# Splitting the last output projection of a state-space mixer around the first cross-attention tiles, and moving two LayerNorms two tiles later

## The chip, the cores and the metric

The kernel runs on one core of a Trainium2 chip. The metric is device time in microseconds (us) of the whole launch, the median of several runs. A core has four computing engines, each with its own instruction queue worked off in order: TensorE (PE in the profile; its weight loads are PEld), VectorE (DVE), ScalarE (ACT) and GpSimd (POOL). SyncE (SP) only issues transfers here. Engines wait for each other through semaphores.

## What is computed

A decoder layer with post-normalisation over x of shape (2, 2048, 512) in float32: a state-space mixer, a cross attention on a context of 77 rows, and a feed-forward part in which 16 slots per batch attend to all tokens, pass through 16 experts, and are attended to by the tokens.

```python
x = _layernorm(x + mixer(x, W_in, conv_w, conv_b, A_param, dt_bias, W_out))
x = _layernorm(x + cross_attention(x, ctx_1024, q_w, ..., o_b))
x = _layernorm(x + slots_and_experts(x, slot_query, ..., e_b2))
```

The end of the mixer is `out.reshape(b, s, -1) @ W_out.T`, then residual and LayerNorm. In the cross attention, `q = x @ q_w + q_b` with 16 heads of 32 columns, softmax over the 77 rows of context under a causal mask, the weighted values, and `@ o_w + o_b`, again with residual and LayerNorm.

## The kernel before, in words

The sequence of 2048 is cut into 16 chunks of 128 positions (`CHUNKS`, numbered 0 to 15; `END` is 15), and a chunk covers both batches (`BATCH` is 2). The cross attention goes over 32 tiles of 128 tokens: tiles 0 to 15 are batch 0, tiles 16 to 31 batch 1. The program is one block in which each engine's order is written out by hand in `cross_rows`: first a Python loop over chunks 0 to 14 of the mixer, then a hand-ordered seam that mixes the end of chunk 15 with the start of tiles 0 and 1, and then `tiles(engine, step)`, which calls `step(t, ...)` for every tile. Tiles 0 to `MIXER_OVER` are written out one by one, then a hardware loop takes two tiles per turn up to tile 13, then four tiles are written out, then a second loop and the last two tiles.

Mixer parts at the seam (`mixer_parts`). `project_out` (line 776) multiplies the rated output of a chunk with W_out, one group of matrix products per batch; for chunk 15 the two results lie in the PSUM banks that the cross stage calls TO (batch 0) and SLOT (batch 1). `residual` (line 834) adds x on DVE, once per batch, and counts `res_done`. `norm` computes mean and reciprocal deviation of a chunk for both batches on DVE: two bn_stats (line 602), then a chain of tiny operations, each waiting for the last (lines 615 to 631 and 842). `normalise` (line 796) applies them on ACT with two activations; `store` (line 713) writes the chunk to memory on SP's queue, from where `load` (line 941) fetches the tiles.

Cross parts of a tile t, in the order of the dependencies: `turn_x1` (PE, 959), `take_x1T` (ACT, 1062), `queries` (PE, 968), `take_queries` (DVE, 1126), `score` (PE, 981), `take_scores` (DVE: maximum 1118 and subtraction 1120, with a mask addition 1115 at tiles 0 and 16 alone), `exponents` (ACT, 1066), `denominators` (DVE: sum 1148, reciprocal 1151), `normalise` (POOL, 1189), `turn_probs` (PE, 988), `take_probsT` (ACT, 1090), `weigh_values` (PE, 997), `take_yT` (ACT, 1106), `project_out` (PE, 1007), `residual` (DVE, 1175), `norm` (DVE, 643 to 660), `scale_rows` (ACT, 1096), `turn_x2` (PE, 1028), `take_x2T` (ACT, 1072), `slot_scores` (PE, 1036), `slot_maxima` (DVE, 1135 to 1144), `slot_exponents` (ACT, 1079 and 1082), `turn_slots` (PE, 1044), `take_slotsT` (ACT, 1101), `weigh_tokens` (PE, 1056), `add_tokens` (DVE, 1163).

They are software-pipelined. `step(t)` on DVE is: `add_tokens(t-2)`, `take_queries(t+1)`, `take_scores(t+1)`, `slot_maxima(t-1)`, `denominators(t+1)`, `slot_sums(t-1)`, `residual(t)`, `norm(t)`. On ACT it begins with `take_probsT(t)` and ends with `scale_rows(t)`. On PE it begins with `turn_probs(t)`, `turn_x1(t+2)`, `weigh_values(t)`, `turn_x2(t-1)`, `score(t+1)`, and ends with `queries(t+2)` and `weigh_tokens(t-1)`. On POOL it is `add_bias(t+1)` and `normalise(t+1)`.

In the kernel before, both batches of the last `project_out` come right before tile 0's `turn_probs` on PE; both residuals and the norm of chunk 14 come right before `step(0)` on DVE, and the norm of chunk 15 in `step(1)`, after `take_queries(2)`. The rows of chunks 14 and 15 are scaled on ACT in steps 1 and 2 (`LATE_ROWS`) and stored in steps 2 and 3 (`LATE_STORES`). After the tiles, the experts stream their weights (2 MB units) from memory.

Of the kernel before, what the change touches and what calls it, by code (L numbers as in the profile page):

```python
# [24 lines left out]
BATCH, SEQ, D = 2, 2048, 512  # L25
TOKENS = BATCH * SEQ
TILES = TOKENS // P
CHUNKS = SEQ // P
# [117 lines left out]
def wait_later(eng, sem, value):  # L146

    if not isinstance(value, int) or value > 0:
        eng.wait_ge(sem, value)
# [522 lines left out]
def mixer_parts(nc, io, hold, st):  # L672
# [96 lines left out]
                                        start=False, stop=True, skip_group_check=True)  # L769
        last.then_inc(s["y_done"], 1)  # L770

    def project_out(pe, c):
        for b in range(BATCH):
            pe.wait_ge(s["yT_done"], 2 * c + b + 1)
            for g in range(GROUPS):
                last = nc.tensor.matmul(outputs(c)[b], yT[:, b, g * P:(g + 1) * P], wout[:, g, :], start=(g == 0), stop=(g == GROUPS - 1))  # L776
            last.then_inc(s["out_done"], 1)
# [47 lines left out]
        for b in range(BATCH):  # L825
            nc.vector.tensor_tensor(yT[:, b, :], Y[:], rateT[c % 2][:, b * GROUPS:(b + 1) * GROUPS, :].rearrange("p g t -> p (g t)"), ALU.mult).then_inc(s["yT_done"], 1)  # L826

    def residual(dve, c):
        u = c % 2
        dve.wait_ge(x_arrived[u], 16 * (c // 2 + 1))  # L830
        wait_later(dve, s["x1_done"], c - 1)
        for b in range(BATCH):
            dve.wait_ge(s["out_done"], 2 * c + b + 1)
            nc.vector.tensor_tensor(xr[u][:, b, :], outputs(c)[b], x_in[u][:, b, :], ALU.add).then_inc(s["res_done"], 1)  # L834

# [44 lines left out]

MIXER_OVER = 7
LATE_ROWS = {1: CHUNKS - 2, 2: CHUNKS - 1}
LATE_STORES = {2: CHUNKS - 2, 3: CHUNKS - 1}
SLOT_WEIGHTS = {4: ("dwv", "d_Wv"), 5: ("dwo", "d_Wo")}
FIRST_UNITS = {6: 0, 7: 1, CHUNKS - 2: 2, CHUNKS - 1: 3, CHUNKS: 4, CHUNKS + 1: 5}


def tokens_stage(nc, io, hold, ring, ring_in):  # L890
# [10 lines left out]
def cross_rows(nc, io, hold, ring, ring_in, st, first, slots, combine):  # L901
# [26 lines left out]
    mix = hold["mix"]  # L928
# [43 lines left out]
    def score(pe, t, b):  # L972

        pe.wait_ge(s["qT_done"], t + 1)
        if isinstance(t, int) and t == 0:
            pe.wait_ge(mix["scores_masked"], HG * CHUNKS)
        wait_later(pe, s["prT_done"], HG * t)
        for g in range(GROUPS):
            for h in range(HG):
                r = slice(h * HD, (h + 1) * HD)  # L980
                last = nc.tensor.matmul(SC[:, h, g * CTX:(g + 1) * CTX], qT[r, g, :], hold["k"][r, b, g, :], start=True, stop=True)  # L981
        last.then_inc(s["sc_done"], 1)
# [18 lines left out]
    def project_out(pe, t):  # L1001
        pe.wait_ge(s["yT_done"], t + 1)
        if isinstance(t, int) and t == 0:
            pe.wait_ge(mix["res_done"], BATCH * CHUNKS)
        wait_later(pe, s["x2T_done"], t)
        for k in range(KC):
            last = nc.tensor.matmul(TO[:], yT[:, k, :], wo[:, k, :], start=(k == 0), stop=(k == KC - 1))  # L1007
        last.then_inc(s["o_done"], 1)
# [22 lines left out]
    def slot_scores(pe, t, u):  # L1031
        pe.wait_ge(s["x2T_done"], t + 1)
        wait_later(pe, s["slot_exp"], t)
        for m in range(SM):
            for k in range(KC):
                last = nc.tensor.matmul(slot_bank(t)[:, m * P:(m + 1) * P], hold["m1"][:, k, m * P:(m + 1) * P], x2T[u][:, k, :],  # L1036
                                        start=(k == 0), stop=(k == KC - 1))
        last.then_inc(s["slot_sc"], 1)
# [168 lines left out]
    def before(t, tiles):  # L1207

        return not isinstance(t, int) or t >= tiles
# [7 lines left out]
    with nc.Block() as block:  # L1217
# [51 lines left out]
        def _(pe):  # L1269
# [18 lines left out]
            first["weigh_steps"](pe, END)  # L1288
            score(pe, 0, 0)
            queries(pe, 1)  # L1290
            first["project_out"](pe, END)

            def step(t, u, half, seq):
                turn_probs(pe, t)
                if ahead(t, 2):
                    turn_x1(pe, t + 2, u, half + 1)
                if at_end(t):
                    slots["keep_busy"](pe, 4, 5)
                weigh_values(pe, t, seq(0))
                if before(t, 1):  # L1300
                    turn_x2(pe, t - 1, 1 - u)
                if at_end(t):
                    slots["keep_busy"](pe, 2, 5)
                    project_out(pe, t)
                    slot_scores(pe, t - 1, 1 - u)
                    return
                if ahead(t, 1):
                    score(pe, t + 1, seq(1))
                if before(t, 1):
                    slot_scores(pe, t - 1, 1 - u)  # L1310
                project_out(pe, t)
                if before(t, 1):
                    turn_slots(pe, t - 1)
                if ahead(t, 2):
                    queries(pe, t + 2)
                if before(t, 1):
                    weigh_tokens(pe, t - 1, 1 - u)
# [74 lines left out]
        def _(dve):  # L1392
# [28 lines left out]
            take_scores(dve, 0, True)  # L1421
            denominators(dve, 0)
            take_queries(dve, 1)
            first["residual"](dve, END)
            first["norm"](dve, END - 1)

            def step(t, u, half, seq):
                if before(t, 2):
                    add_tokens(dve, t - 2, seq(-2))
                if ahead(t, 1) and before(t, 1):  # L1430
                    take_queries(dve, t + 1)
                if isinstance(t, int) and t == 1:
                    first["norm"](dve, END)
                if isinstance(t, int) and t == LAST - 1:
                    slots["invert_sums"](dve, 0)
                    for m in range(SM):
# [8 lines left out]
                    take_scores(dve, t + 1, isinstance(t, int) and (t + 1) % CHUNKS == 0)  # L1445
                if before(t, 1):
                    slot_maxima(dve, t - 1, seq(-1))
                if ahead(t, 1):
                    denominators(dve, t + 1)
                if before(t, 1):  # L1450
# [953 lines left out]
```

## Time and profile before

| | us |
|---|---|
| median of 3 runs | 1537.43 (1537.12 to 1540.24) |
| the profiled execution | 1536.38 |
| its span, first to last instruction | 1534.7 |
| busy in it: PE | 1389.1 (91%) |
| DVE | 801.5 (52%) |
| ACT | 444.5 (29%) |
| POOL | 216.9 (14%) |

The span falls into stages: the mixer with its tables up to about 410 us, the seam, the tiles up to about 939 us, the experts up to about 1390 us, where the transfer engines are full for most of the time, and the last attention to the end. In a timeline a row gives start, duration, engine, line, operation, the tensors written and read, the count, and in brackets how long the engine was idle before it and what ended that. Tensors lie in large arenas, so they are told apart by line, not by name. A row with a count merges instructions, and its duration runs from the start of the first to the end of the last.

### The profile page before, as it was taken

The numbers are of one execution on the slowest core, as the hardware profiler recorded it, in microseconds if no ns is written. First come the engines' busy times: TensorE is split into PE (matmuls) and PEld (weight loads), VectorE is DVE, ScalarE is ACT, GpSimd is POOL, SyncE is SP. The second block draws the span as 40 slices with busy tenths as digits, with TensorE's granted clock in tenths as the row PEclk, the third lists the DMA queues.
The fourth block names the chain that finished last, engine by engine and source line by source line (L and its number), as shares of the span: only waits on it lengthen the run. The fifth ranks groups of instructions, "written<-read, shape, count | busy, mean of one in ns | idle before, by whom it ended". The sixth has DMA issues, their size and how long they took to land.

```text
span 1534.7 us, 26475 instructions
## 1 busy us (share of the span) xinstructions
PE 1389.1 (91%) x10067; PEld 864.6 (56%) x10067; DVE 801.5 (52%) x2168; ACT 444.5 (29%) x934; POOL 216.9 (14%) x181
## 2 busy tenths in 40 slices
PE   7899999999999999999999999886776776779997
PEld 4677777777667777777777776221111111127664
DVE  1656676777787767677676774000000000005997
ACT  2434334334144444444444442000000000002332
POOL 1111110011031212212121211000000000001221
PEclk9999999999999999999999999887778888789999
DMA  9543133132212241144111136999999999994663
GB/s 344 170 125 97 56 97 97 43 96 83 83 35 84 97 168 46 48 165 152 62 41 52 51 148 242 414 426 424 427 427 426 427 427 427 423 423 162 206 206 137
DMA packets 74860, 309.31 MB, mean 202 GB/s; under 512 B 8907, under 2 KB 14155, under 8 KB 56984
## 3 DMA queue, kind: packets, MB, share of 16 engines
q1 hardware_dynamic: 72344, 293.49, 49.7%
q10 hardware_dynamic: 2432, 14.68, 2.7%
q8 instruction: 55, 0.90, 0.2%
q14 instruction: 29, 0.24, 0.0%
HBM read 274.33 MB, written 33.82 MB: 201 GB/s over the span
## 4 chain that ended last, share of the span: by engine, by line
PE 49%; DMA 21%; DVE 17%; issue 4%; ACT 3%; POOL 0%; DVEq 0%; ACTq 0%; POOLq 0%
DMA all_ring<-in_e_Wg 21%; PE mix_bank L968 7%; PE mix_bank L1007 7%; PE mix_bank L177 4%; PE mix_scores L1611 4%; PE mix_bank L1036 4%; PE mix_bank L1056 3%; PE mix_scores L988 3%; DVE all_ring L247 3%; PE mix_scores L981 2%; PE mix_bank L997 2%; PE mix_scores L1632 2%; DVE all_ring L602 1%; PE mix_bank L1028 1%; DVE all_ring L834 1%
## 5 line engine op out<-in xcount | busy, mean ns | idle before, releaser
L1611 PE MATMUL mix_scores<-all_ring,all_space 128*32 128x512 f32 x960 | 150.6, 722 | 74.4 <-DMA all_ring<-in_e_Wg 37.6
L1659 DVE TENSOR_TENSOR all_space<-all_space 128x512 f32<-128x512 f32 x16 | 11.1, 694 | 379.3 <-ACT all_space L1668 379.3
L177 PE MATMUL mix_bank<-all_ring,all_space 128*128 128x256 f32 x672 | 157.1, 388 | 3.5 <-POOL all_ring L1472 3.5
L177 PEld LDWEIGHTS mix_bank<-all_ring,all_space 128*128 128x128 f32 x672 | 127.1, 193 | 29.9 <-issue 9.0
L1668 ACT ACTIVATE all_space<-mix_scores 128x512 f32<-128x512 f32 x32 | 19.1, 597 | 408.0 <-PE mix_scores L1618 408.0
L1611 PEld LDWEIGHTS mix_scores<-all_ring,all_space 128*32 128x32 f32 x960 | 31.3, 120 | 176.1 <-DMA all_ring<-in_e_Wg 67.2
L1632 PE MATMUL mix_scores<-all_ring,all_space 128*32 128x512 f32 x496 | 119.1, 762 | 11.0 <-DVE all_space L1662 11.0
L1189 POOL TENSOR_TENSOR all_space<-all_space 128x1232 f32<-128x1232 f32 x32 | 72.2, 2256 | 396.2 <-DVE all_space L1151 396.2
L968 PE MATMUL mix_bank<-all_space 128*128 128x128 f32 x1024 | 119.8, 276 | 0.0
L968 PEld LDWEIGHTS mix_bank<-all_space 128*128 128x128 f32 x1024 | 116.9, 192 | 0.7 <-issue 0.5
L1007 PE MATMUL mix_bank<-all_space 128*128 128x512 f32 x256 | 115.3, 594 | 0.3 <-ACT all_space L1072 0.3
L247 DVE SCALAR_TENSOR_TENSOR all_ring<-all_ring,all_space 128x256 f32<-128x256 f32 x192 | 84.4, 482 | 52.9 <-ACT all_ring L196 50.4
L776 PE MATMUL mix_scores<-all_space,all_ring 128*128 128x512 f32 x240 | 105.5, 593 | 0.8 <-DVE all_ring L826 0.8
L1118 DVE TENSOR_REDUCE all_space<-mix_scores 128x16 f32<-128x1232 f32 x30 | 43.3, 1442 | 94.5 <-PE mix_scores L981 94.5
L1632 PEld LDWEIGHTS mix_scores<-all_ring,all_space 128*32 128x32 f32 x496 | 28.2, 136 | 89.5 <-issue 73.9
L776 PEld LDWEIGHTS mix_scores<-all_space,all_ring 128*128 128x128 f32 x240 | 45.6, 190 | 52.0 <-issue 50.2
L1007 PEld LDWEIGHTS mix_bank<-all_space 128*128 128x128 f32 x256 | 46.2, 191 | 46.4 <-issue 46.4
L1066 ACT ACTIVATE all_space<-all_space 128x1232 f32<-128x1232 f32 x32 | 39.3, 1230 | 113.0 <-DVE all_space L1120 113.0
L988 PEld LDWEIGHTS mix_scores<-all_ident,all_space 128*77 128x77 f32 x512 | 58.2, 148 | 18.5 <-issue 15.4
L1090 ACT ACTIVATE all_space<-mix_scores 77x512 f32<-77x512 f32 x128 | 65.1, 588 | 10.2 <-PE mix_scores L988 9.9
L1096 ACT ACTIVATE all_space<-all_space 128x512 f32<-128x512 f32 x32 | 26.1, 816 | 138.6 <-DVE all_space L660 138.6
L1036 PE MATMUL mix_bank<-all_space 128*128 128x128 f32 x512 | 65.6, 281 | 0.1
(309 smaller groups left out, 2239.5 us busy)
## 6 DMA issues: line engine op xcount, KB each, us to landing
all_ring<-in_e_W SPq DMA_DIRECT2D x55, 2048.0 KB, 24.7
all_ring<-in_e_Wg SPq DMA_DIRECT2D x29, 2048.0 KB, 26.2
all_ring<-in_e_W ACTq DMA_DIRECT2D x5, 2048.0 KB, 8.9
all_ring<-in_xT SPq DMA_DIRECT2D x8, 1024.0 KB, 9.2
all_ring<-scratch_rates SPq DMA_DIRECT2D x64, 128.0 KB, 4.1
all_z<-in_x SPq DMA_DIRECT2D x16, 512.0 KB, 3.9
all_space<-scratch_x SPq DMA_DIRECT2D x32, 256.0 KB, 2.8
scratch_x<-all_space SPq DMA_DIRECT2D x32, 256.0 KB, 2.0
```

The lines of the kernel that those rows point to most:

```text
L177: last = nc.tensor.matmul(bank[:, i * BT:(i + 1) * BT], hold["win"][:, k, m * P:(m + 1) * P], hold["xT"][b % 2][:, k, :], start=(k == 0), ...
L247: last = nc.vector.scalar_tensor_tensor(conv[:, m0 + i, :], proj[:, m0 + i, k:k + BT], taps[:, m0 + i, k:k + 1], conv[:, m0 + i, :], ALU.m ...
L776: last = nc.tensor.matmul(outputs(c)[b], yT[:, b, g * P:(g + 1) * P], wout[:, g, :], start=(g == 0), stop=(g == GROUPS - 1))
L968: last = nc.tensor.matmul(AV[:, g * P:(g + 1) * P], wq[:, k, g * P:(g + 1) * P], x1T[:, k, :], start=(k == 0), stop=(k == KC - 1))
L988: last = nc.tensor.transpose(SC[0:CTX, g, h * P:(h + 1) * P], pr[:, h * GROUPS + g, :], hold["ident"][:])
L1007: last = nc.tensor.matmul(TO[:], yT[:, k, :], wo[:, k, :], start=(k == 0), stop=(k == KC - 1))
L1036: last = nc.tensor.matmul(slot_bank(t)[:, m * P:(m + 1) * P], hold["m1"][:, k, m * P:(m + 1) * P], x2T[u][:, k, :], start=(k == 0), stop=( ...
L1056: nc.tensor.matmul(to[:], sp_prT[:, m * P:(m + 1) * P], x2[u][:], start=True, stop=True).then_inc(s["z_done"], 1)
L1090: nc.scalar.activation(prT[:, g * HG:(g + 1) * HG, :].rearrange("p h t -> p (h t)"), SC[0:CTX, g, :], ACT.Copy).then_inc(s["prT_done"], 1)
L1189: nc.gpsimd.tensor_tensor(pr[:], pr[:], broadcast(rden[:].unsqueeze(2), [P, HEADS, CTX]), ALU.mult).then_inc(s["normed"], 1)
L1611: last = nc.tensor.matmul(bank[w][q * ROWS:(q + 1) * ROWS, :], hm[u][:, k, :], weights[k % 2][:, q * FQ:(q + 1) * FQ], start=(k == 0), sto ...
L1632: return nc.tensor.matmul(bank[3][q * ROWS:(q + 1) * ROWS, :], guT[:, i, q * ROWS:(q + 1) * ROWS], weights[q % 2][:, i * D:(i + 1) * D], s ...
```

## The change

PE issues batch 0's part of the last output projection in the old place and batch 1's part in step 0, after the scores of tile 1. DVE does batch 0's residual in the old place and batch 1's in step 0, after `take_scores(1)`. The two norms of chunks 14 and 15 leave the seam and step 1, and go into steps 2 and 3, between `slot_maxima` and `denominators`. The rows are then scaled in steps 3 and 4 and stored in steps 4 and 5. Two weight transfers of the slot stage, issued by ACT, move from steps 4 and 5 to 6 and 7, two prefetches of expert weights from 6 and 7 to 8 and 9, and tiles 8 and 9 leave the loop. Two waits follow the banks: tile 0's projection waits for 31 residuals instead of 32, and the first slot scores wait for all 32.

```diff
-    def project_out(pe, c):
-        for b in range(BATCH):
+    def project_out(pe, c, batches=range(BATCH)):
+        for b in batches:
...
-    def residual(dve, c):
+    def residual(dve, c, batches=range(BATCH)):
...
-        for b in range(BATCH):
+        for b in batches:
...
-MIXER_OVER = 7
-LATE_ROWS = {1: CHUNKS - 2, 2: CHUNKS - 1}
-LATE_STORES = {2: CHUNKS - 2, 3: CHUNKS - 1}
-SLOT_WEIGHTS = {4: ("dwv", "d_Wv"), 5: ("dwo", "d_Wo")}
-FIRST_UNITS = {6: 0, 7: 1, CHUNKS - 2: 2, CHUNKS - 1: 3, CHUNKS: 4, CHUNKS + 1: 5}
+MIXER_OVER = 9
+LATE_NORMS = {2: CHUNKS - 2, 3: CHUNKS - 1}
+LATE_ROWS = {3: CHUNKS - 2, 4: CHUNKS - 1}
+LATE_STORES = {4: CHUNKS - 2, 5: CHUNKS - 1}
+SLOT_WEIGHTS = {6: ("dwv", "d_Wv"), 7: ("dwo", "d_Wo")}
+FIRST_UNITS = {8: 0, 9: 1, CHUNKS - 2: 2, CHUNKS - 1: 3, CHUNKS: 4, CHUNKS + 1: 5}
...
-            pe.wait_ge(mix["res_done"], BATCH * CHUNKS)
+            pe.wait_ge(mix["res_done"], BATCH * CHUNKS - 1)
...
+        if isinstance(t, int) and t == 0:
+            pe.wait_ge(mix["res_done"], BATCH * CHUNKS)
...
-            first["project_out"](pe, END)
+            first["project_out"](pe, END, [0])
...
+                if isinstance(t, int) and t == 0:
+                    first["project_out"](pe, END, [1])
...
-            first["residual"](dve, END)
-            first["norm"](dve, END - 1)
+            first["residual"](dve, END, [0])
...
-                if isinstance(t, int) and t == 1:
-                    first["norm"](dve, END)
...
+                if isinstance(t, int) and t == 0:
+                    first["residual"](dve, END, [1])
+                if isinstance(t, int) and t in LATE_NORMS:
+                    first["norm"](dve, LATE_NORMS[t])
```

## Rows read from the trace of the kernel before

**Rows 1.** Windows: stretch, length, busy per engine, granted clock, DMA share, GB/s.

```profile
474.00:490.00 16.00, 16.00 (x155) 12.42 (x153) 11.72 (x32) 7.14 (x16) 3.48 (x2) 1.00 0.24 83
1020.00:1060.00 40.00, 31.09 (x170) 7.72 (x168) 3.58 (x8) 1.79 (x3) 0.00 (x0) 0.74 1.01 427
```

**Rows 2.** Timeline of PE at the seam.

```profile
420.52 7.03 PE L776 MATMUL mix_bank<-all_space,all_ring 128*128 128x512 f32 x16
427.39 1.91 PE L988 MATMUL mix_scores<-all_ident,all_space 128*77 128x128 f32 x16
...
430.68 1.13 PE L981 MATMUL mix_scores<-all_space 32*128 32x77 f32 x32
...
435.28 3.73 PE L968 MATMUL mix_bank<-all_space 128*128 128x128 f32 x32
440.58 1.97 PE L988 MATMUL mix_scores<-all_ident,all_space 128*77 128x128 f32 x16 [1.57 <-POOL all_space L1189]
...
445.48 0.66 PE L1028 MATMUL mix_bank<-all_ident,all_space 128*128 128x128 f32 x4
```

**Rows 3.** Timeline of DVE at the seam.

```profile
428.20 1.28 DVE L602 BATCH_NORM_STATS2 all_ring<-all_ring 128x6 f32<-128x512 f32 x2
...
432.26 1.44 DVE L1118 TENSOR_REDUCE all_space<-mix_scores 128x16 f32<-128x1232 f32 x1
...
438.11 0.63 DVE L1175 TENSOR_TENSOR all_space<-mix_bank,all_space 128x512 f32<-128x512 f32 x1
```

**Rows 4.** Timelines of POOL (L1189) and ACT at the seam.

```profile
424.61 2.25 POOL L1189 TENSOR_TENSOR all_space<-all_space 128x1232 f32<-128x1232 f32 x1 [18.41 <-DVE all_space L1151]
...
442.33 0.81 ACT L1096 ACTIVATE all_space<-all_space 128x512 f32<-128x512 f32 x1 [5.89 <-DVE all_space L660]
443.05 2.02 ACT L1090 ACTIVATE all_space<-mix_scores 77x512 f32<-77x512 f32 x4
```

**Rows 5.** Timeline of DVE from step 2 into step 3.

```profile
466.99 0.17 DVE L1144 COPY all_top<-all_space 128x2 f32<-128x2 f32 x1
467.25 1.44 DVE L1148 TENSOR_REDUCE all_space<-all_space 128x16 f32<-128x1232 f32 x1
...
473.31 1.40 DVE L1163 SCALAR_TENSOR_TENSOR all_z<-all_z,all_space,mix_bank 128x512 f32<-128x512 f32 x2
...
478.81 1.44 DVE L1118 TENSOR_REDUCE all_space<-mix_scores 128x16 f32<-128x1232 f32 x1 [3.50 <-PE mix_scores L981]
```

**Rows 6.** Timelines of POOL, ACT and PE from step 2 into step 3.

```profile
469.06 2.26 POOL L1189 TENSOR_TENSOR all_space<-all_space 128x1232 f32<-128x1232 f32 x1 [12.29 <-DVE all_space L1151]
...
473.43 0.82 ACT L1096 ACTIVATE all_space<-all_space 128x512 f32<-128x512 f32 x1 [4.40 <-DVE all_space L660]
474.43 2.04 ACT L1090 ACTIVATE all_space<-mix_scores 77x512 f32<-77x512 f32 x4 [0.18 <-PE mix_scores L988]
...
481.76 1.23 ACT L1066 ACTIVATE all_space<-all_space 128x1232 f32<-128x1232 f32 x1 [3.44 <-DVE all_space L1120]
...
457.96 1.91 PE L988 MATMUL mix_scores<-all_ident,all_space 128*77 128x128 f32 x16
...
473.74 1.91 PE L988 MATMUL mix_scores<-all_ident,all_space 128*77 128x128 f32 x16
...
477.02 0.66 PE L1028 MATMUL mix_bank<-all_ident,all_space 128*128 128x128 f32 x4
```

**Rows 7.** Timelines at step 15: queries on PE in steps 14 and 15, DVE's mask.

```profile
657.93 3.74 PE L968 MATMUL mix_bank<-all_space 128*128 128x128 f32 x32
...
675.06 3.74 PE L968 MATMUL mix_bank<-all_space 128*128 128x128 f32 x32
...
668.30 1.44 DVE L1115 TENSOR_TENSOR all_space<-mix_scores,all_space 128x1232 f32<-128x1232 f32 x1 [3.51 <-PE mix_scores L981]
```

**Rows 8.** Timelines at chunk 13's norm on DVE, and POOL beside it.

```profile
405.08 1.13 DVE L629 SCALAR_TENSOR_TENSOR all_ring<-all_ring 128x2 f32<-128x2 f32 x1
...
404.92 1.27 POOL L1185 TENSOR_TENSOR all_space<-all_space 128x512 f32<-128x512 f32 x1 [40.86 <-DMA all_space<-in_o_b]
```

## The prediction

> **What bounds the kernel now.** The page's busy times come first (the table above): TensorE is busy 91% of the span, so it is the engine to follow. The windows then say where it has no room: in the tiles of the cross stage it is busy 16.00 of 16.00 us with DVE at 11.72, while among the experts it is busy 31.09 of 40 and the transfer engines are full [rows 1]. The change touches the seam and the tiles up to tile 9. Two questions follow. What idle time of PE is there to win at the seam, and how much later may DVE be in a tile before PE feels it?
>
> For the first, PE's timeline at the seam. After the last output projection (420.52 to 427.5) it runs on until tile 1's `turn_probs`, before which it stands 1.57 us for POOL; the next rows hold another pause of under 1 us, for ACT's four copies of the turned probabilities [rows 2]. So all that could be won at the seam is some 2.4 us, under 0.2% of the kernel.
>
> For the second, DVE's timeline in a tile. It stands 3.50 us before `take_scores` [rows 5]. That looks like room for a norm of 4 us with little over. But idle time in front of one instruction is room only for work that stands in front of that instruction. What matters for the two norms is how long PE can wait for the work queued behind them: `denominators(t+1)`, `residual(t)`, `norm(t)`, and in the next step `add_tokens` and `take_queries`.
>
> **Part 1: the split projection.** Batch 1's half of 7.03 us, 3.44 us up to the start of the next work (6.87 from 420.52 to 427.39, halved) leaves the place ahead of `turn_probs(0)` and stands behind `score(1)` [rows 2]. `turn_probs(0)` also needs POOL's `normalise(0)`, which ends at 426.86 [rows 4]. So PE, done with batch 0 at 423.96, starts tile 0 at 426.9 instead of 427.39: 0.5 us earlier, with a new pause of 2.9 us. `score(1)` starts at 430.2 and ends at 431.3. DVE is then free, since norm 14 no longer stands ahead of it, and starts `take_scores(1)` at 431.4 instead of 432.26 [rows 3]. PE does batch 1's projection 431.26 to 434.70. DVE, done with the subtraction 2.91 us after 431.4, at 434.3, waits for it 0.4 us and adds the residual until 435.5, which is when ACT's exponentials end: they took until 436.44 before, and move with `take_scores` by 0.86. What is queued behind this new wait, the denominators, loses nothing. POOL would let `turn_probs(1)` go at 440.58, where it released it before [rows 2], less 0.86, near 439.8.
>
> But PE itself is not there by then. Without its pause it would have started `turn_probs(1)` at 440.58 - 1.57 = 439.01 [rows 2]; now it starts at 439.01 - 0.5 + 3.44 = 441.95. That is 1.4 us later than before: the pause was moved from in front of tile 1 to in front of tile 0, and grew. Part of it comes back at once. The path that ended last before was DVE's residual(0) and norm(0) at 438.11, `scale_rows(0)` on ACT at 442.33, then the four copies at 443.05, behind which `weigh_values(1)` ended and `turn_x2` began at 445.48 [rows 2 to 4]. In the new order tile 0's projection ends at 435.28 + 3.44 - 0.5 = 438.2, so residual(0) starts some 0.2 us later than 438.11, and so do all that follow. PE's 441.95 is still in time for that: its first turned quarter is there at about 442.6, ahead of ACT's 443.3. So the seam costs +0.2 us. Bounds: -2.4 (every pause gone) and +1.4 (nothing of PE's delay comes back). I take 0.2, since ACT's copies are the row that PE leaned on before.
>
> **Part 2: the two norms.** Norm 14 took 428.20 to 432.26, 4.06 us [rows 3]. Before, it stood where DVE otherwise would have waited, at a cost of at most 0.4 us, and norm 15 stood in step 1 in the same way. Taking them out gives DVE room in the seam and in step 1, which part 1 has already used up. Put back in step 2, a norm stands between `slot_maxima`, which ends at 467.16, and the sum of the exponentials, which starts at 467.25 [rows 5]. So everything from that sum on is late by 4.06 - 0.09 = 3.97 us. What of it PE can bear, path by path:
> - through POOL: `normalise(3)` ends at 471.32, `turn_probs(3)` starts at 473.74 [rows 6], room 2.4. PE is 1.6 us late there.
> - through DVE to ACT: norm(2) ends, ACT scales at 473.43 and starts its copies at 474.43 after 0.18 idle [rows 6]. Back to back the distance of the two is 0.72 to 0.89 (442.33 to 443.05 at the seam [rows 4]), so the room here is 0.11 to 0.28. From the first copy to `turn_x2` are 2.43 us where ACT paces them (443.05 to 445.48 [rows 2, 4]), and 2.59 here (474.43 to 477.02 [rows 6]): another 0.16. The room of the whole path is about 0.3, and 3.97 - 0.3 = 3.7 us arrive at PE.
> - `add_tokens(1)`, which gives back the bank that `turn_x1(5)` writes, and `take_queries(4)` come right behind the norm from 473.31 on [rows 5] and hold PE by a little less than the 3.7.
>
> The step then closes its circle: `turn_x2`, `score(4)` and DVE's `take_scores(4)` all start 3.7 us late, DVE has again stood idle before it, and step 3 begins as step 2 did, with PE aligned. Norm 15 costs the same once more. Sum of part 2: 2 x 3.7 = 7.4 us.
>
> There is a row that shows the same thing in small. At step 15 DVE has one more operation, the mask addition of 1.44 us, and PE's queries come 675.06 - 657.93 = 17.13 us after those of step 14 [rows 7], against 15.78 from tile to tile from `turn_probs(2)` to `turn_probs(3)` (473.74 less 457.96 [rows 6]). 1.44 us more on DVE made PE 1.35 us late although DVE had 3.51 idle right before. Bounds of part 2: twice POOL's 1.6, 3.2 us, and twice the whole norm with no room at all, 8.1.
>
> Here a rule of the Trainium skill speaks against the change. One tiny operation of chunk 13's norm took 1.13 us for two columns, where a whole norm takes 4.06, and POOL's addition of 1.27 us ran from 404.92 to 406.19 beside it [rows 8]. The page "SBUF — State Buffer", section "SBUF: two separate sides", says that a DVE operation with two SBUF inputs and a GpSimd operation that reads SBUF take a shared pair of ports in turns, and the later one is blocked; the trace agrees. By that rule each late norm could pay some 1.1 us more, and the sum would be 2.2 higher. At 467 to 471 us POOL does nothing until 469.06 [rows 6], and what it does there waits for the denominators behind the norm, so I put it at zero.
>
> **Part 3: the rest.** ACT's two activations for the rows move to steps 3 and 4, in front of the exponentials, where ACT stands idle for 3.44 us [rows 6]; cost 0. Stores, two weight transfers and two prefetches move by two tiles, queued where they were queued before, and nobody waits for them before the experts; cost 0, bounds -0.4 to +0.4 for the issue on ACT. Two tiles more written out and one loop turn less: PE was full in either form, so 0, bounds -0.3 to +0.3. If ACT's room were gone, 1.5 us each would be due.
>
> After the tiles the expert weights stream at 427 GB/s [rows 1]. The stream's start hangs on the end of the tiles, so a delay of these goes through whole.
>
> **The sum.** 0.2 + 7.4 = 7.6 us. The profiled execution took 1536.38 (span 1534.7); it would take 1544.0. The median of the runs lies 1.05 above it, so 1545.0.
>
> **The rivals.**
> A. The norms are hidden after all, and the kernel isn't slower. DVE is busy some 12.3 of 15.8 us per tile (3.50 idle [rows 5]); a norm makes 16.3, only 0.6 over. If the room stood on the path through POOL and ACT as it stands before `take_scores`, the cost would be 2 x 0.6 + 0.2 = 1.4, so 1538.8. It decides at a room of 3.5 us between norm(t) on DVE and ACT's copies; the rows show 0.3. Chance 0.06.
> B. Only POOL's path counts, because ACT takes the copies before it scales, or because the delay is caught up: 2 x 1.6 + 0.2 = 3.4, so 1540.8. Against it: ACT's order is written out, and step 15 lost nearly all of its 1.44. Chance 0.06.
> C. The clock. PE has pauses of up to 2.9 us at the seam and several between 0.5 and 1.6 in tiles 3 and 4. The granted clock was 1.00 in the tiles and 0.74 where PE was idle for 9 of 40 us [rows 1]. If some 18 us of tiles ran at 0.74, that would add 18 x 0.35 = 6, so 1551. Against it: the pauses at the seam before, 1.57 us the longest, cost no clock. The Trainium skill, "TensorE: Matmul & The Clock Gate", section "HAM oscillation — how this bites in real kernels", says that idle gaps of PE send its clock to half until it is busy again; no stretch here is as idle as the experts'. Chance 0.05.
> D. The seam wins its 2.4 and A holds without its 1.2: 1535.0, within 0.2%. For more than that nothing in the rows has the size. Chance 0.02 to be over 0.2% faster, another 0.01 here.
> My forecast has the remaining 0.80.
>
> **Range and chances.** Runs of this kernel differ by up to 3 us, and about 0.2% (3.1 us) is what a measurement can tell from no change. Forecast with its bounds: 1542 to 1547. To 8 in 10 I widen it to 1541.0 (near B) and 1548.5 (ports, part of C). Faster 0.02; same, from A and D, 0.07; slower, from the forecast, B and C, 0.91.
>
> **What would show it.** PE in step 0: a pause of about 2.9 us before `turn_probs(0)`, none before `turn_probs(1)`. In steps 2 and 3 DVE runs a norm between `slot_maxima` and the sum; in steps 3 and 4 PE pauses, in several pieces, for 3.7 us in all, the last for ACT's copies, and `score` follows the last one by 19.5 us instead of 15.8, twice. All later tiles keep 15.8. ACT's L1096 loses its lead over L1090. I am wrong if PE's distance from tile 2 to tile 3 or 3 to 4 stays under 17 us, if the seam gains over 1 us, or if the experts' stream starts less late than the tiles end.

## The result and the profile after

| | before | after |
|---|---|---|
| median, us | 1537.28 (1534.74 to 1540.24, 6 runs) | 1547.78 (1544.72 to 1550.41, 6 runs) |
| ratio | | 1.0061, 95% interval 1.0042 to 1.0079 |
| profiled execution | 1536.38 | 1550.41 |
| its span | 1534.7 | 1548.3 |
| first expert bias on TensorE starts at | 950.93 | 963.21 |

The change makes the kernel 10.5 us slower, with an interval of about 6.5 to 12. The forecast was 7.6 us slower (1545.0, range 1541.0 to 1548.5). The two profiled executions differ by 14.0 us. Of that, 1.16 us lie before anything that the change touches: the last scores of the mixer (L746) start at 408.57 and at 409.73. Then 11.1 us arise between there and the first expert, which starts 12.28 us later. Another 1.3 us come behind, in the experts and the last attention, whose code is the same, and the last 0.4 lie outside the span (14.0 against 1548.3 - 1534.7 = 13.6). So 11.1 is the number to explain.

The lines of the kernel after are shifted by one to six against those of before: `turn_probs` is L989 (988 before), `turn_x1` L960, `weigh_values` L998, `turn_x2` L1029, `score` L982, `slot_scores` L1039, `project_out` of the tiles L1008, `weigh_tokens` L1059; on DVE the maximum is L1121, the sum L1151, the cross residual L1178, `add_tokens` L1166; on ACT `scale_rows` is L1099 and the four copies L1093; on POOL `normalise` is L1192.

PE's timeline at the seam, kernel after (start, duration, engine, line; in brackets the idle time before it), which answers to [rows 2]:

```profile
409.73 1.17 PE L746 MATMUL mix_scores<-all_ring 32*128 32x128 f32 x32 [0.22 <-DVE all_ring L834]
...
421.68 3.60 PE L776 MATMUL mix_bank<-all_space,all_ring 128*128 128x512 f32 x8
428.06 2.68 PE L989 MATMUL mix_scores<-all_ident,all_space 128*77 128x128 f32 x16 [2.78 <-POOL all_space L1192]
430.53 1.06 PE L960 MATMUL mix_bank<-all_ident,all_space 128*128 128x128 f32 x4
431.52 1.57 PE L998 MATMUL mix_bank<-all_space 77*32 77x128 f32 x32
433.02 1.13 PE L982 MATMUL mix_scores<-all_space 32*128 32x77 f32 x32
434.08 3.70 PE L776 MATMUL mix_bank<-all_space,all_ring 128*128 128x512 f32 x8
...
444.62 1.91 PE L989 MATMUL mix_scores<-all_ident,all_space 128*77 128x128 f32 x16
...
448.69 0.66 PE L1029 MATMUL mix_bank<-all_ident,all_space 128*128 128x128 f32 x4
...
464.46 0.66 PE L1029 MATMUL mix_bank<-all_ident,all_space 128*128 128x128 f32 x4
...
505.01 0.66 PE L1029 MATMUL mix_bank<-all_ident,all_space 128*128 128x128 f32 x4
...
520.78 0.66 PE L1029 MATMUL mix_bank<-all_ident,all_space 128*128 128x128 f32 x4
```

The pause is where the prediction put it: 2.78 us before `turn_probs(0)`, none before `turn_probs(1)`. But the same work then takes longer. `turn_probs(0)` needs 2.68 us where it needed 1.91 [rows 2], the four transposes behind it (L960) 1.06 instead of the 0.60 of L959 before. From the mixer's last scores to `turn_x2` it is 448.69 - 409.73 = 38.96 us, against 445.48 - 408.57 = 36.91 before: +2.05.

DVE's timeline in step 2 and into step 3, kernel after, which answers to [rows 5]:

```profile
470.19 0.17 DVE L1147 COPY all_top<-all_space 128x2 f32<-128x2 f32 x1
470.27 1.29 DVE L602 BATCH_NORM_STATS2 all_ring<-all_ring 128x6 f32<-128x512 f32 x2
...
474.26 0.16 DVE L842 SCALAR_TENSOR_TENSOR all_ring<-all_ring 128x2 f32<-128x2 f32 x1
474.34 1.43 DVE L1151 TENSOR_REDUCE all_space<-all_space 128x16 f32<-128x1232 f32 x1
...
480.39 1.40 DVE L1166 SCALAR_TENSOR_TENSOR all_z<-all_z,all_space,mix_bank 128x512 f32<-128x512 f32 x2
...
486.73 1.44 DVE L1121 TENSOR_REDUCE all_space<-mix_scores 128x16 f32<-128x1232 f32 x1 [4.34 <-PE mix_scores L982]
```

ACT (first two lines) and PE in step 3, kernel after, which answer to [rows 6]:

```profile
480.51 0.81 ACT L1099 ACTIVATE all_space<-all_space 128x512 f32<-128x512 f32 x1 [8.28 <-DVE all_space L660]
481.23 2.03 ACT L1093 ACTIVATE all_space<-mix_scores 77x512 f32<-77x512 f32 x4
...
476.97 1.13 PE L1059 MATMUL mix_bank<-all_space 128*128 128x512 f32 x2 [0.72 <-DVE all_space L1178]
478.45 1.97 PE L989 MATMUL mix_scores<-all_ident,all_space 128*77 128x128 f32 x16 [0.35 <-POOL all_space L1192]
481.89 0.63 PE L960 MATMUL mix_bank<-all_ident,all_space 128*128 128x128 f32 x4 [1.47 <-issue]
482.45 1.28 PE L998 MATMUL mix_bank<-all_space 77*32 77x128 f32 x32
483.67 1.06 PE L1029 MATMUL mix_bank<-all_ident,all_space 128*128 128x128 f32 x4
484.66 2.01 PE L982 MATMUL mix_scores<-all_space 32*128 32x77 f32 x32
486.59 3.78 PE L1039 MATMUL mix_bank<-all_space 128*128 128x128 f32 x16
```

The norm stands between the slot maxima and the sum: the sum now starts 4.15 us behind the copy L1147, 0.26 before [rows 5], so it and all behind it is 3.89 us late. DVE still stands idle for 4.34 us ahead of L1121, so its norm wasn't hidden in that. PE waits in four pieces: for the residual (0.72), for POOL (0.35), for `add_tokens` (1.47, where the trace names no releaser, but L1166 ends at 481.79, just ahead), and inside `weigh_values`, which takes 1.28 instead of 1.08 because it is paced by ACT's copies. Measured from the `turn_x2` before, PE is 1.50 us later than in the kernel before at `turn_probs(3)`, 3.20 at `turn_x1(5)` and 3.44 at the next `turn_x2`. Then a second effect sets in: from L1029 on matrix products take nearly twice as long, 2.01 for 1.13 and 3.78 for 2.05.

Windows of the kernel after (stretch, length, busy PE, PEld, DVE, ACT, POOL, then the granted clock, DMA share, GB/s):

```profile
424.00:432.00 8.00, 5.22 (x35) 3.78 (x38) 2.78 (x4) 2.64 (x5) 3.48 (x2) 0.82 0.12 33
482.00:490.00 8.00, 8.00 (x88) 6.90 (x89) 3.27 (x3) 4.66 (x9) 0.00 (x0) 0.61 0.28 100
```

Both stretches lie behind pauses of PE, and the mean granted clock in them is between 1.00 and 0.50, the shares of its two levels, 2.4 and 1.2 GHz: part of the time it was at the lower one. The same stretches in the kernel before:

```profile
424.00:432.00 8.00, 8.00 (x94) 5.60 (x93) 5.59 (x22) 3.12 (x6) 3.48 (x2) 1.00 0.11 33
482.00:490.00 8.00, 8.00 (x49) 5.75 (x48) 7.25 (x27) 2.96 (x8) 3.48 (x2) 1.00 0.03 12
```

**Where the 11.1 us are.** From `turn_x2` to `turn_x2` the steps are 15.77 us apart before. After, they are 15.77 (1 to 2), 19.21 (2 to 3), 21.34 (3 to 4) and 15.77 again (4 to 5). So: seam 2.05, late norm 14 3.44, late norm 15 with the second fall of the clock 5.57. The sum is 11.06. The 15.77 from 4 to 5 also says that the rows' activations of step 4 cost PE nothing, and the next ten distances, 15.77 to 15.82, say so of the transfers that were moved.

### The profile page after: what moved, and what is told of

The parts are those of the page before. It is cut to its first block, busy times and chain, and to the rows that moved or that the text cites. A ratio compares the mean times of both kernels' runs of the same rounds, so it can differ in the third digit from the quotient of the medians.

```text
span 1548.3 us, 26391 instructions
## 1 busy us (share of the span) xinstructions
PE 1395.4 (90%) x10067; PEld 870.1 (56%) x10067; DVE 801.8 (52%) x2168; ACT 445.4 (29%) x934; POOL 216.9 (14%) x181
## 4 chain that ended last, share of the span: by engine, by line
PE 48%; DMA 21%; DVE 18%; issue 4%; ACT 3%; POOL 1%; DVEq 0%; ACTq 0%; POOLq 0%
DMA all_ring<-in_e_Wg 21%; PE mix_bank L969 6%; PE mix_bank L1008 6%; PE mix_bank L177 4%; PE mix_scores L1617 4%; PE mix_bank L1039 4%; PE mix_scores L989 4%; PE mix_bank L1059 3%; DVE all_ring L247 3%; PE mix_scores L982 2%; PE mix_bank L998 2%; PE mix_scores L1638 2%; DVE all_ring L602 1%; PE mix_bank L1029 1%; DVE all_ring L834 1%
## 5 line engine op out<-in xcount | busy, mean ns | idle before, releaser
L1617 PE MATMUL mix_scores<-all_ring,all_space 128*32 128x512 f32 x960 | 149.2, 718 | 78.1 <-DMA all_ring<-in_e_Wg 39.8
L1665 DVE TENSOR_TENSOR all_space<-all_space 128x512 f32<-128x512 f32 x16 | 11.1, 694 | 381.6 <-ACT all_space L1674 381.6
L1192 POOL TENSOR_TENSOR all_space<-all_space 128x1232 f32<-128x1232 f32 x32 | 72.2, 2255 | 407.5 <-DVE all_space L1154 407.5
L1638 PE MATMUL mix_scores<-all_ring,all_space 128*32 128x512 f32 x496 | 117.4, 752 | 11.0 <-DVE all_space L1668 11.0
L1008 PE MATMUL mix_bank<-all_space 128*128 128x512 f32 x256 | 115.4, 594 | 0.3 <-ACT all_space L1075 0.3
L1121 DVE TENSOR_REDUCE all_space<-mix_scores 128x16 f32<-128x1232 f32 x30 | 43.3, 1442 | 105.3 <-PE mix_scores L982 105.3
L1008 PEld LDWEIGHTS mix_bank<-all_space 128*128 128x128 f32 x256 | 46.5, 191 | 47.0 <-issue 47.0
L989 PEld LDWEIGHTS mix_scores<-all_ident,all_space 128*77 128x77 f32 x512 | 58.5, 149 | 21.1 <-issue 14.1
L1093 ACT ACTIVATE all_space<-mix_scores 77x512 f32<-77x512 f32 x128 | 65.5, 588 | 10.1 <-PE mix_scores L989 9.7
L1099 ACT ACTIVATE all_space<-all_space 128x512 f32<-128x512 f32 x32 | 26.1, 816 | 146.5 <-DVE all_space L660 136.7
L1039 PE MATMUL mix_bank<-all_space 128*128 128x128 f32 x512 | 67.3, 285 | 0.1
```

Of the source, the lines that this page charges most:

```text
L989: last = nc.tensor.transpose(SC[0:CTX, g, h * P:(h + 1) * P], pr[:, h * GROUPS + g, :], hold["ident"][:])
L1093: nc.scalar.activation(prT[:, g * HG:(g + 1) * HG, :].rearrange("p h t -> p (h t)"), SC[0:CTX, g, :], ACT.Copy).then_inc(s["prT_done"], 1)
L1192: nc.gpsimd.tensor_tensor(pr[:], pr[:], broadcast(rden[:].unsqueeze(2), [P, HEADS, CTX]), ALU.mult).then_inc(s["normed"], 1)
L1617: last = nc.tensor.matmul(bank[w][q * ROWS:(q + 1) * ROWS, :], hm[u][:, k, :], weights[k % 2][:, q * FQ:(q + 1) * FQ], start=(k == 0), sto ...
L1638: return nc.tensor.matmul(bank[3][q * ROWS:(q + 1) * ROWS, :], guT[:, i, q * ROWS:(q + 1) * ROWS], weights[q % 2][:, i * D:(i + 1) * D], s ...
```

## The experiments

All distances in this table are read from PE's timeline: from the start of L746 to the first `turn_x2`, and from `turn_x2` to `turn_x2` of the steps named.

| kernel | L746 to turn_x2(0) | step 1 to 2 | 2 to 3 | 3 to 4 | 4 to 5 |
|---|---|---|---|---|---|
| before (two profiles) | 36.91, 36.91 | 15.77 | 15.78 | 15.77 | 15.77 |
| after | 38.96 | 15.77 | 19.21 | 21.34 | 15.77 |
| a1, after again | 38.96 | 15.77 | 19.21 | 21.21 | 15.77 |
| a2, seam only | 38.97 | 15.77 | 15.77 | 15.77 | 15.78 |
| a3, norms only | 36.54 | 18.99 | 19.21 | 21.40 | 15.77 |
| c1, a3 again | 36.53 | 18.95 | 19.34 | 21.32 | 15.77 |
| a4, after with all pauses filled | 37.36 | 15.77 | 19.21 | 19.20 | 15.78 |
| d1, only the seam filled | 37.36 | 15.77 | 19.22 | 19.21 | 18.94 |
| d2, only steps 3 and 4 filled | 38.98 | 15.77 | 19.21 | 19.21 | 15.77 |
| c2, a3 with tile 1 filled | 36.53 | 15.77 | 19.19 | 19.20 | 15.77 |
| b1, norms ahead of the scores | 38.97 | 15.77 | 16.13 | 16.24 | 15.77 |

### The change in its parts

Two theories stood against each other: that the order of the queues explains the whole loss, and that the order and the clock do together. The first run is the kernel after once more.

> The changed kernel again, on the chip of the three kernels below. Theory (queue order plus clock): the two late norms cost about 3.5 us each as a delay of what is queued behind them on DVE; PE's pause of 2.8 us before turn_probs(0) and those of step 3 make the granted clock fall for some us afterwards, worth 1.7 to 1.9 us each time. Sum 10 to 11 us over the kernel before; turn_x2 to turn_x2 from tile 2 to 3 about 19.2 us, from 3 to 4 about 21.3 if the clock falls there again and 19.3 if it doesn't. Rival (only the order counts, the slow stretches were chance): the distances are 19.3 and 19.3, the seam +0.2, the sum 7 us.

Measured: 1549.54 us median against 1537.53, ratio 1.0071 (1.0051 to 1.0091). The distances repeat to 0.13 us, and the clock fell in both places again. So the slow stretches were no chance, and the order alone does not explain them.

Seam only (against the kernel after; the constants at the top are those of the kernel before):

```diff
...
             first["residual"](dve, END, [0])
+            first["norm"](dve, END - 1)
...
+                if isinstance(t, int) and t == 1:
+                    first["norm"](dve, END)
...
-                if isinstance(t, int) and t in LATE_NORMS:
-                    first["norm"](dve, LATE_NORMS[t])
```

> Only the split of the last output projection and of the residual; norm 14 right behind batch 0's residual, where DVE now waits for tile 1's scores, norm 15 in step 1, all constants as before. Order alone: +0.2 us, since PE's pause goes from before tile 1 to before tile 0. Order plus clock: +0.2 and about 1.8 for the clock after the new pause of 2.8 us, so +2.0; the granted clock between turn_probs(0) and score(1) is under 1. Rival (the split helps, as the pause of 1.57 us is gone): -1.5 to -2.4.

Measured: 1539.89 against 1537.53, ratio 1.001 (0.9997 to 1.0022). The time alone can't tell it from no change, but its interval leaves no room for a gain of 1.5 us. The distance is +2.06, and the granted clock from 428 to 432 us is 0.66:

```profile
428.00:432.00 4.00, 3.79 (x28) 3.44 (x32) 3.30 (x17) 2.46 (x5) 1.39 (x2) 0.66 0.20 66
```

The split brings nothing: the rival is wrong.

Norms only (against the kernel before; the constants at the top are those of the kernel after):

```diff
...
             first["residual"](dve, END)
-            first["norm"](dve, END - 1)
...
-                if isinstance(t, int) and t == 1:
-                    first["norm"](dve, END)
...
+                if isinstance(t, int) and t in LATE_NORMS:
+                    first["norm"](dve, LATE_NORMS[t])
```

> Only the two norms moved to steps 2 and 3, in front of the denominators; projection and residuals unsplit as before, stores and prefetches as in the changed kernel. Order alone: 2 x 3.5 = +7 us, with step 0 a little better (take_scores(1) 0.4 us earlier as norm 14 is gone from in front of it), so +6.6. Order plus clock: +6.6 to +8.6, as the clock falls in one of the two tiles. Rival (the norms are hidden in DVE's idle 3.5 us, and the loss is the seam's): +1.

Measured: 1549.94 against 1537.53, ratio 1.0076 (1.0055 to 1.0097), +12.4, far above what either form of the theory gave. Where it comes from stands in the table. The seam is 0.37 us better, as expected. The steps 2 to 3 and 3 to 4 are those of the kernel after. New is step 1 to 2, 18.99 instead of 15.77, where no norm stands late. Its two pauses, and the windows behind them:

```profile
444.36 1.97 PE L989 MATMUL mix_scores<-all_ident,all_space 128*77 128x128 f32 x16 [1.19 <-POOL all_space L1190]
...
447.55 1.78 PE L998 MATMUL mix_bank<-all_space 77*32 77x128 f32 x32 [0.79 <-ACT all_space L1091]
```


```profile
440.00:448.00 8.00, 6.03 (x61) 5.40 (x63) 5.96 (x18) 2.10 (x5) 5.22 (x3) 1.00 0.04 12
448.00:451.00 3.00, 2.88 (x48) 1.98 (x52) 0.00 (x0) 2.50 (x5) 0.00 (x0) 0.81 0.17 63
451.00:456.00 5.00, 5.00 (x34) 4.56 (x32) 3.28 (x3) 1.12 (x1) 0.00 (x0) 0.50 0.31 105
```

The clock fell behind tile 1's two pauses, 1.19 and 0.79 us, for 3.2 us of loss. So a fall may follow pauses that the kernel before has too, and they needn't be long.

### The clock

Filling the pauses of the kernel after with products of no use (`keep_busy` multiplies the identity with itself; its first number is how many):

```diff
+            pe.wait_ge(mix["yT_done"], 2 * CHUNKS)
+            slots["keep_busy"](pe, 10, 5)
...
                 turn_probs(pe, t)
+                if isinstance(t, int) and t in (3, 4):
+                    slots["keep_busy"](pe, 5, 5)
```

> The changed kernel, with matrix products of no use in PE's pauses: ten of 128 x 128 before turn_probs(0), some 2.7 us, and five behind turn_probs(3) and turn_probs(4), some 1.3 us each; they delay nothing that isn't waiting anyway. Order plus clock: the granted clock stays at 1.00 from 424 us on, and the time falls from the changed kernel's by 3.5 us, to +7 over the kernel before. Order alone: no change against the changed kernel (+-0.5).

Measured: 1543.13 against 1537.53, ratio 1.0032 (1.0018 to 1.0046). That is 6.4 us less than the kernel after on the same chip, while the distances say 1.6 + 2.1 = 3.7; the medians of the two have some 2 us of noise each, so I go by the distances. The work that waits is the same (19.21 and 19.20), and only the clock differs. Its timeline at the seam:

```profile
424.76 2.39 PE L1784 MATMUL mix_bank<-all_ident 128*128 128x128 f32 x20
427.72 1.97 PE L989 MATMUL mix_scores<-all_ident,all_space 128*77 128x128 f32 x16 [0.56 <-POOL all_space L1192]
```

And its windows:

```profile
424.00:432.00 8.00, 7.44 (x107) 6.41 (x105) 2.44 (x4) 3.12 (x6) 3.47 (x2) 1.00 0.11 33
482.00:490.00 8.00, 8.00 (x72) 5.79 (x71) 6.11 (x18) 4.81 (x11) 0.00 (x0) 1.00 0.20 68
```

With 1.00 in both windows, this kernel's distances are the pure price of the order: seam 37.36 - 36.91 = +0.45, norms 3.44 and 3.43. The sum is 7.3 us, and its first expert bias starts 959.02 - 409.38 = 549.64 us behind L746, against 542.36 before: +7.28.

Does the fall belong to tile 1's pauses, and is it chance?

> The kernel with the norms alone once more, one profile. If the fall of the clock behind tile 1's two pauses (1.19 and 0.79 us) belongs to this order of work, turn_x2(0) to turn_x2(1) is 19.0 us again and tile 3 to 4 21.4. If it is chance (the same pauses, somewhat longer ones even, cost the kernel before nothing in two profiles), it is 15.8 here, or the fall comes elsewhere.

Measured (one run each): 1550.67 against 1541.60. 18.95 and 21.32: the same falls in the same places.

> The kernel before, one more profile. It has the same two pauses in tile 1 (1.57 and 0.78 us) as the kernel with the norms alone (1.19 and 0.79), where the clock fell for 3.2 us' worth. If the fall hangs on when the pause comes and not on its length alone, it may show here; if length decides, the clock stays at 1.00 as in the first profile.

Measured: 36.91 and a clock of 1.00 up to 520 us in this profile too, with pauses of 1.56 and 0.79. So both kernels repeat themselves, and the length of the pauses doesn't decide between them, as the kernel without a fall has the longer one.

> The norms alone, with products of no use in tile 1's two pauses (four and two of 128 x 128), nothing in tiles 3 and 4. If the pauses made the clock fall, turn_x2(0) to turn_x2(1) is 15.8 us, tile 2 to 3 stays at 19.2, and tile 3 to 4 at 21.4. Rival (the fall in tile 1 has nothing to do with the pauses): 19.0 still.

```diff
+                if isinstance(t, int) and t == 1:
+                    slots["keep_busy"](pe, 4, 5)
                 turn_probs(pe, t)
...
+                if isinstance(t, int) and t == 1:
+                    slots["keep_busy"](pe, 2, 5)
```

These lines are what it adds to the kernel with the norms alone (a3). Measured (one run each): 1543.55 against 1541.60. Tile 1's fall is gone, as expected. The expectation for tile 3 to 4 missed: 19.20 instead of 21.4. Nothing was filled there; its pauses are 0.72, 0.35 and 1.47 us like those of the kernel after, but the clock stayed at 1.00. That suggested that the second fall is an echo of the first, which the next two kernels ask.

> The changed kernel with the ten products of no use before turn_probs(0) alone; tiles 3 and 4 pause as they do in the changed kernel. If the fall in tile 3 follows from the earlier one at the seam (filling tile 1's pauses in the kernel with the norms alone took away both), the granted clock is 1.00 throughout, turn_x2(0) comes 37.4 us after the last mixer scores, and the tile distances are 19.2 and 19.2. If tile 3's own pauses decide, tile 3 to 4 is 21.2.

Measured (one run each): 1549.54 against 1540.48. With the seam filled, step 3 to 4 is 19.21, but the fall has come one step later: 4 to 5 is 18.94, and the granted clock there:

```profile
500.00:512.00 12.00, 10.53 (x96) 8.37 (x95) 6.61 (x14) 7.46 (x14) 0.00 (x0) 0.72 0.32 111
```

> The changed kernel with the products in tiles 3 and 4 alone; the seam pauses 2.8 us. The fall at the seam stays (turn_x2(0) 39.0 us after the last mixer scores), and that in tile 3 is gone as its longest pause is filled: 19.2 and 19.2. If the fall in tile 3 is only the seam's echo, 21.2 from tile 3 to 4 in spite of the filling.

Measured (one run each): 1549.33 against 1540.48. The seam falls, 38.98; steps 3 and 4 don't, 19.21 and 19.21. So the second fall is no mere echo: it goes when its own pauses are filled, although the seam's fall is still there. But c2 and d1 show that its own pauses are not enough either: with the same pauses unfilled, and the earlier fall taken away, it was absent or came one step later. Put together: in all five profiles in which PE stood idle for 2.8 us before `turn_probs(0)` the clock fell behind it, and in both where this was filled it didn't. Behind the smaller pauses of tiles 1, 3 and 4 it fell in some orders of work and not in others, each time at a price of 2.0 to 3.2 us. What decides there is open. A moment that depends on what PE did before is compatible with d1 and c2, but no run varied the moment alone.

### The place of the norm

If what is queued behind an operation counts, the same norms in the same tiles cost next to nothing when they stand ahead of the scores.

```diff
                 if ahead(t, 1) and before(t, 1):
                     take_queries(dve, t + 1)
+                if isinstance(t, int) and t in LATE_NORMS:
+                    first["norm"](dve, LATE_NORMS[t])
...
-                if isinstance(t, int) and t in LATE_NORMS:
-                    first["norm"](dve, LATE_NORMS[t])
```

> The changed kernel with the two norms still at steps 2 and 3, but ahead of take_scores, in the 3.5 us for which DVE waits for the scores there, instead of in front of the denominators. Theory (what is queued behind counts): the norm of 4.0 us overruns the wait by 0.5 us; PE has 0.1 to 0.4 us of room for that, so turn_x2 to turn_x2 is 15.9 to 16.3 us from tile 2 to 3 and 3 to 4, not 19.2 and 21.3, and the clock doesn't fall there. With the seam's +2.0 (0.45 for the order, 1.6 for the clock) the sum is +2.3 to +3.0 over the kernel before. Rival (DVE's busy time counts, the place doesn't): the distances stay at 19.2 and more and the sum at +11.

Measured: 1539.49 against 1538.14, ratio 0.9998 (0.9982 to 1.0014). The distances are as expected, 16.13 and 16.24 in place of 19.2 and 21.3:

```profile
462.39 0.65 PE L1029 MATMUL mix_bank<-all_ident,all_space 128*128 128x128 f32 x4
478.52 0.66 PE L1029 MATMUL mix_bank<-all_ident,all_space 128*128 128x128 f32 x4
494.76 0.66 PE L1029 MATMUL mix_bank<-all_ident,all_space 128*128 128x128 f32 x4
```

From L746 to the first expert bias this profile has 545.20 us, +2.84; the timed ratio lies a little below that, and its interval ends at +2.2. DVE does exactly the same work as in the kernel after. The place is worth 3.08 us for the first norm and 5.10 for the second (with its clock), 8.2 of the 11.1 us.

How large is the room in front of the denominators? One more sum, in the kernel before, in steps 4 to 7:

```diff
+                if isinstance(t, int) and t in (4, 5, 6, 7):
+                    dve.wait_ge(s["exp_done"], t + 2)
+                    nc.vector.tensor_reduce(top[:], pr[:], AX.X, ALU.add)
```

> The kernel before with one more sum over the probabilities on DVE, 1.44 us, into a tile that nobody reads then, in front of the denominators of steps 4 to 7. Theory: the room there is 0.44 us (3.89 us of late norm made PE 3.44 late), so four tiles take 15.77 + 1.47 - 0.44 = 16.8 us each, sum +4.1. Rival (the room is POOL's 2.4 us, and long norms cost by a threshold): 15.77 each, +0.

Measured: 1541.86 against 1538.14, ratio 1.0022 (1.0 to 1.0043). Its `turn_x2` and, below, DVE in step 4:

```profile
494.32 0.66 PE L1028 MATMUL mix_bank<-all_ident,all_space 128*128 128x128 f32 x4
510.99 0.66 PE L1028 MATMUL mix_bank<-all_ident,all_space 128*128 128x128 f32 x4
527.67 0.65 PE L1028 MATMUL mix_bank<-all_ident,all_space 128*128 128x128 f32 x4
...
500.31 1.44 DVE L1450 TENSOR_REDUCE all_space<-all_space 128x16 f32<-128x1232 f32 x1
501.67 1.43 DVE L1148 TENSOR_REDUCE all_space<-all_space 128x16 f32<-128x1232 f32 x1
```

Four distances of 16.67 to 16.68: each sum shifts the next by 1.36 and PE by 0.90. The room is 0.46 us, where the two norms gave 3.89 - 3.44 = 0.45. There is no threshold at POOL's 2.4 us.

### A version of its own

Norm 14 ahead of the last residuals instead of behind them, so that DVE runs it while PE still projects, with tile 1's pauses filled as in c2:

```diff
+            first["norm"](dve, END - 1)
             first["residual"](dve, END)
-            first["norm"](dve, END - 1)
```

> The kernel before with norm 14 ahead of the last two residuals instead of behind them, so that DVE runs it while PE still projects, and products of no use (four and two of 128 x 128) in PE's two pauses of tile 1. Theory: take_scores(1) starts 0.4 us earlier and all after it too; the pauses shrink by that; sum -0.4 us, turn_x2(0) 36.5 us after the last mixer scores instead of 36.9, and no fall of the clock in tile 1. Rival: the later residuals hold tile 0's projection, +0.3.

Measured: 1537.56 against 1538.14, ratio 0.9988 (0.9973 to 1.0004): no difference that the runs can tell. The distance is 36.53, 0.38 less than before, as expected. It is the distance of a3 (36.54), which fills nothing, so the gain is the order's and the filling costs nothing. What the clock would do here without the filling was not tried. Against the kernel before it stands at 0.9988 where the kernel after stands at 1.0061 and 1.0071, so it beats that by 0.7 to 0.8%. Nearly all of this is what the kernel after loses (11.06 us by the distances), and only 0.38 us is won.

## Why the prediction was right, and where it was off

**What bounds the kernel**: held. Idle time in front of an instruction is no room for work behind it; b1 shows it with the same work in both places.

**Part 1, the split**: the mechanism held step by step: pause of 2.78 (2.9 foretold), none before tile 1, and most of PE's delay given back by ACT's copies (in a4 it is 1.28 us at `turn_probs(1)` and 0.45 at `turn_x2`; 1.4 and 0.2 were foretold). The 0.2 was too small because it took 435.28, the start of the next instruction, for the end of tile 0's projection, which lasts until 435.44; `residual(0)` began 0.38 us later than before, and it and its norm took 0.07 longer. The remaining 1.6 us of the measured 2.05 are the clock, which I had at zero here because the pauses at the seam before had cost no clock. I made that pause longer in my own sum and did not ask again.

**Part 2, the norms**: 2 x 3.7 foretold, 2 x 3.44 measured. The shift was 3.89 (3.97 foretold) and the room 0.45 (0.3 foretold). The 0.15 lies in the step from `scale_rows` to the copies: back to back it is 0.72 us here too, the lower end of my 0.72 to 0.89, and I had worked with the upper. The path is the one named: ACT's L1099 and L1093 are back to back in step 3, and `weigh_values` is paced by the copies. Step 15's mask, which made PE 1.35 late for 1.44, was a fair sign of the direction but hangs on another path: PE waits there 1.14 us for ACT's slot exponentials (L1082), which are queued behind `take_scores`. The room in front of the denominators is 0.46 (b2).

**The shared ports**: POOL had nothing running beside the late norms, which took 4.15 us each from L1147 to the sum. That the bound was left out of the sum was right.

**Part 3**: held; ACT's activations cost PE nothing in steps 3 and 4, the moved transfers neither. The delay of the tiles went through whole: +12.28 at the first expert bias, 13.6 at the end of the span, the difference inside what the experts' part varies by (from the first expert bias to the end of the span: 583.8 and 584.3 us in the two profiles of before, 585.1 and 586.9 in those of after, 581.6 to 587.8 in all fourteen profiles).

**The sum**: order 0.45 + 3.44 + 3.44 = 7.3 against 7.6 foretold. What was missing is the clock, 1.6 + 2.1 = 3.7. It was rival C, with a chance of 0.05 and a price of 6: too low a chance and too high a price. The step that failed was the argument that no stretch here is as idle as the experts'. The rows gave no ground for a bound of that kind; they showed two pauses that had cost nothing and nothing on longer ones.

**What was luck**: the forecast with its own bounds was 1542 to 1547, and 1547.78 lies above that. It is inside the stated range only because this had been widened for the ports and part of the clock. The distances' 11.06 us on top of 1537.43 would give 1548.5, the very edge. The direction and the 7.3 us of the order were foreseen; that the whole came out inside the range was not worked out.

Of what I named as signs against me, none came: the seam didn't gain, no distance stayed under 17 us, and the stream started as late as the tiles ended. Of the signs for me, the distance of 19.5 us came once (19.21); the second one was 21.34, by the clock. Rival A is ruled out by a3 (its norms were not hidden), B by the 3.44, D by a2.

## What to carry to other kernels

When work is moved on an engine that is not the bound, read not how long it stands idle but where: follow what is queued behind the new place to the bounding engine, and count the room on each of the paths, since the smallest decides (here 0.45 us beside 4.3 us of idle time). A pause of TensorE that is only moved or split may still cost clock behind it; compare durations of the same instruction before and after, and price the pause with and without a fall. Where a pause can't be removed, filling it with products of no use took away the fall behind it in each of the four kernels that had one (a4, c2, d1, d2), but in d1 a later fall only came one step later: judge by the whole stage.

## What the runs showed of the hardware

- The granted clock fell behind pauses of 1.19 and 0.79 us in one order of work (3.2 us lost) and did not behind 1.57 and 0.78 in another, each the same in two profiles. Behind one pause of 2.8 us it fell five times in five.
- A DVE operation with a single SBUF operand waited for POOL too, as far as its times tell. In b3 norm 14 runs beside POOL and takes 5.2 us instead of 4.06. DVE's L622, an integer shift of two columns, lasts until POOL's addition is over (428.66 and 428.62) and takes 1.20 us where it takes 0.17 elsewhere, and L620 lasts until POOL's product before it is over (427.42 and 427.41). The shift of a single column, L651, takes its usual 0.15 us in the middle of a product of POOL (L1189, 438.44 to 440.69):

```profile
427.13 0.29 DVE L620 TENSOR_TENSOR all_ring<-all_ring 128x2 f32<-128x2 f32 x1
427.46 1.20 DVE L622 TENSOR_SCALAR all_ring<-all_ring 128x2 int32<-128x2 int32 x1
...
440.20 0.15 DVE L651 TENSOR_SCALAR all_space<-all_space 128x1 int32<-128x1 int32 x1
...
425.16 2.25 POOL L1189 TENSOR_TENSOR all_space<-all_space 128x1232 f32<-128x1232 f32 x1 [17.00 <-DVE all_space L1151]
427.36 1.26 POOL L1185 TENSOR_TENSOR all_space<-all_space 128x512 f32<-128x512 f32 x1
...
438.44 2.25 POOL L1189 TENSOR_TENSOR all_space<-all_space 128x1232 f32<-128x1232 f32 x1 [9.81 <-DVE all_space L1151]
```

The Trainium skill, "SBUF — State Buffer", section "SBUF: two separate sides", names for a DVE operation that takes the shared ports either two SBUF inputs or a mode that uses two ports. L620 fits the first, and L622 fits only if it ran in the second, which no row here shows.
